# Gate and up on whole-number weights, with the scales applied when a bank is read, and down two tiles behind

## What is computed

```
xn = layernorm(x)                                  # 2048 rows of 512
s  = attention(xn)                                 # q, k, v projection, clip, layer norm of q and k,
                                                   # 32 heads of 16, ALiBi, causal softmax, output projection
W  = (imatrix - zeros) * scales                    # imatrix: integers 0..15; zeros and scales: one row per 128 input rows
g  = silu( (silu(xn @ W_gate) * (xn @ W_up)) @ W_down )     # 512 -> 1792 -> 512
out = x + s * g
```

## Time and profile before

| | us |
|---|---|
| median of 3 runs | 1297.69 (1294.58 to 1305.38) |
| span of the profiled execution | 1300.7 |
| stage 1, projection of q, k, v (to about 205) | 205 |
| stage 2, attention and weight jobs (about 205 to 764) | 559 |
| stage 3, output projection and feed-forward (about 764 to 1300.7) | 537 |
| TensorE busy | 1205.7 (93%) |
| VectorE busy | 754.4 (58%) |
| ScalarE busy | 626.0 (48%) |
| GpSimd busy | 503.3 (39%) |

### The profile page before, as it was taken

How to read it: one execution, slowest core, us unless ns; L and a number is a source line. 1 busy time by engine, 2 the same in 40 slices (tenths; PEclk the granted TensorE clock), 3 DMA queues, 4 the chain that set the end, 5 groups by cost and what they waited for, 6 DMA issues and landing times. The chain is left out here.

```text
span 1300.7 us, 23572 instructions
## 1 busy us (share of the span) xinstructions
PE 1205.7 (93%) x6848; PEld 768.9 (59%) x6848; DVE 754.4 (58%) x1835; ACT 626.0 (48%) x955; POOL 503.3 (39%) x544
## 2 busy tenths in 40 slices
PE   6999987999999899899998989999999999999997
PEld 5777752333333333333333358887888888888886
DVE  6877887877877778778777622225222522252223
ACT  3333332666666566566665764335433443344332
POOL 2755550313131221212131333555455445545553
PEclk9999986999999999999999989999999999999999
DMA  6234454454546444555565210001100010011000
GB/s 222 91 115 131 138 163 133 116 144 105 147 105 143 99 118 84 125 107 149 107 149 108 83 69 1 1 1 40 57 0 0 32 65 0 0 33 65 1 1 33
DMA packets 101901, 106.62 MB, mean 82 GB/s; under 512 B 28385, under 2 KB 81121, under 8 KB 101729
## 3 DMA queue, kind: packets, MB, share of 16 engines
q1 hardware_dynamic: 75392, 93.10, 27.7%
q10 hardware_dynamic: 26464, 12.98, 3.4%
HBM read 84.41 MB, written 21.23 MB: 81 GB/s over the span
## 5 line engine op out<-in xcount | busy, mean ns | idle before, releaser
L842 ACT ACTIVATE pr<-pair 128x1024 f32<-128x1024 f32 (+3 forms) x384 | 293.6, 811 | 179.7 <-PE pair L965 101.3
L1089 POOL TENSOR_TENSOR ws_lo<-w_f,ws_hi 128x512 fp32r<-128x512 f32 x168 | 238.0, 1445 | 271.8 <-ACT ws_hi L1130 271.8
L264 DVE CUSTOM_DVE_ANT_0 bank<-bank,sg 128x384 f32<-128x384 f32 (+3 forms) x512 | 242.3, 515 | 97.7 <-PE bank L274 94.4
L1251 DVE TENSOR_TENSOR sg<-pair,sg 128x512 f32<-128x512 f32 x56 | 38.8, 692 | 276.0 <-ACT sg L1188 276.0
L1318 PE MATMUL pair<-xc_hi,ws_lo 128*128 128x512 f32 x448 | 175.4, 392 | 0.0
L1318 PE MATMUL pair<-xc_lo,ws_hi 128*128 128x512 f32 x448 | 175.2, 391 | 0.0
L1318 PE MATMUL pair<-xc_hi,ws_hi 128*128 128x512 f32 x448 | 175.1, 391 | 0.0
L267 DVE TENSOR_REDUCE mx<-bank 128x1 f32<-128x512 f32 x256 | 159.8, 683 | 7.4 <-PE bank L274 6.7
L1188 ACT ACTIVATE sg<-pair 128x512 f32<-128x512 f32 x56 | 33.5, 598 | 235.7 <-PE pair L1318 235.6
L799 POOL TENSOR_TENSOR w_f<-w_f,zst 128x896 f32 (+1 forms) x24 | 50.1, 2088 | 215.2 <-ACT zst L856 215.2
L274 PE MATMUL bank<-xin_c,s_sb 108*128 108x512 bf16 (+3 forms) x384 | 118.3, 354 | 13.1 <-DVE mx L264 10.2
(11 more groups left out here) (101 smaller groups left out, 1980.0 us busy)
## 6 DMA issues: line engine op xcount, KB each, us to landing
stk<-parts ACTq DMA_DIRECT2D x16, 768.0 KB, 5.9
zst<-in_z_all SPq DMA_DIRECT2D x24, 448.0 KB, 4.2
sst<-in_s_all SPq DMA_DIRECT2D x24, 448.0 KB, 5.0
w_f<-in_w_all SPq DMA_DIRECT2D x24, 448.0 KB, 6.8
xin_c<-in_x SPq DMA_DIRECT2D x32, 256.0 KB, 2.7
s_sb<-stk SPq DMA_DIRECT2D x96, 64.0 KB
xin_c<-stk SPq DMA_DIRECT2D x96, 64.0 KB
qs<-stk SPq DMA_DIRECT2D x96, 64.0 KB
```

The lines of the kernel that those rows point to most:

```text
L264: dve.tensor_tensor_reduce(out=src, in0=src, in1=tri[:, 512 - w:512], scale=1.0, scalar=-3.0e38, op0=ALU.add, op1=ALU.max, accum_out=dst). ...
L842: act.activation(pr[e % 3][:, 2 * p:2 * p + 2, 0:w], pair[p][:, :, 0:w], ACT.Exp, scale=SCALE)\
L1089: return pool.tensor_tensor(dst, src, hi.bitcast(F32), ALU.subtract)
L1251: dve.tensor_tensor(sg[s][:, :], pair[s][:, 1, :], sg[s][:, :], ALU.mult).then_inc(h_mul, 1)
```

## The change

**Gate and up.** The half jobs of gate and up no longer multiply by the scales: GpSimd subtracts the zeros and writes the whole numbers (-15 to 15) straight into a tile of type F32R, `w_gu`, which holds them without a rest. Only down's weights (`w_d`) are still scaled. The scale DMA of those 16 of the 24 half jobs is gone (`sst` now takes their raw integers). `gate_up` is 2 matmuls for each projection and contraction tile, `xc_lo` and `xc_hi` against the same whole-number weights: 16 a tile of 128 channels in place of 24. Each of the 8 partial sums of a tile has a PSUM bank of its own, in a ring of four (`GB`), because its scale differs. The scale is a number per partition there, from a small tile `sgu` that stage 1 makes (one DMA, one transpose, one copy). The first contraction tile's sum is read by ScalarE (`first`: copy with scale into `acc`), the other three by VectorE (`add`: bank times scale plus `acc`, a scalar_tensor_tensor). silu and the product (`gate`) then work on `acc` in SBUF.

**Down.** `h_lo` is made on GpSimd (`h_low`) in place of VectorE, and of the weights only down's piece is split in stage 3 (one ScalarE copy and one GpSimd subtraction a tile in place of three each). On TensorE `gate_up` is cut in four pairs, and `down` of two tiles before in four quarters; they alternate.

**Around the blocks.** Attention's transposes go through the `y` banks, with split tiles of their own (`of_hi`, `of_lo`), and the output projection's halves stand between the pairs of tiles 0 to 2. xn has four buffers in place of two.

The core of the diff:

```diff
-                def job(jj):
-                    w = w_f[:, bass.ds(jj * HALF, HALF)]
-                    pool.wait_ge(z_conv, jj + 1)
+                def job(ip, n):
+                    w = w_half(ip, n)
+                    pool.wait_ge(z_conv, 3 * ip + n + 1)
                     apart(pool, "pool")
+                    if n < 2:
+                        pool.tensor_tensor(w_gu[:, bass.ds(half_of(ip, n) * HALF, HALF)], w, zst[:, :], ALU.subtract)\
+                            .then_inc(w_ready, 1)
+                        return
                     pool.tensor_tensor(w, w, zst[:, :], ALU.subtract).then_inc(z_sub, 1)
...
-                    pool.tensor_tensor(w, w, sst[:, :], ALU.mult).then_inc(z_mul, 1)
+                    pool.tensor_tensor(w, w, sst[:, :], ALU.mult).then_inc(w_ready, 1)
...
+                def h_low(b, it):
+                    pool.wait_ge(hh_done, IT * b + it + 1)
+                    pool.tensor_tensor(h_lo[it % 3][:, :], acc[0][it % 2][:, :], h_hi[it % 3][:, :].bitcast(F32), ALU.subtract)\
+                        .then_inc(hl_done, 1)
+                def w_low(b, it):
+                    pool.wait_ge(wd_high, IT * b + it + 1)
+                    pool.tensor_tensor(wd_lo[it % 2][:, :], w_down(it), wd_hi[it % 2][:, :].bitcast(F32), ALU.subtract)\
+                        .then_inc(wd_low, 1)
...
+                def first(b, it, n):
+                    act.wait_ge(hl_done, IT * b + it + 1)
+                    act.wait_ge(gu_done, IT * NJ * b + NJ * it + n + 1)
+                    act.activation(acc[n][it % 2][:, :], GB[n], ACT.Copy, scale=scale_of(n, 0, it)).then_inc(ev_first, 1)
...
                 def body(b, last):
...
+                    for it in range(IT + 1):
+                        if it > 0:
+                            silu(b, it - 1)
+                        if 1 <= it <= 2:
+                            copy_s(b, 2 * it - 2)
+                        if it < IT:
+                            for n in range(2):
+                                first(b, it, n)
+                        if it < 2:
+                            hi_o(b, 2 * it)
+                            load_o(b, 2 * it + 1)
+                        if it == 0:
+                            hi_o(b, 1)
+                            load_o(b, 2)
+                        else:
+                            h_high(b, it - 1)
+                            if it <= 2:
+                                copy_s(b, 2 * it - 1)
+                            if it == 1:
+                                hi_o(b, 3)
+                            w_high(b, it - 1)
...
+                def add(b, it, j):
+                    n, k = j % 2, j // 2
+                    dve.wait_ge(gu_done, IT * NJ * b + NJ * it + j + 1)
...
+                    dve.scalar_tensor_tensor(out=a, in0=GB[j % 4], scalar=scale_of(n, k, it), in1=a, op0=ALU.mult, op1=ALU.add)\
+                       .then_inc(ev_add, 1)
...
-                    for g in range(2):
-                        for k in range(KT):
-                            cols = slice(k * P, (k + 1) * P)
-                            for n, (l, r) in enumerate(terms(ws_hi[s][:, g, cols], ws_lo[s][:, g, cols], xc_hi[:, k, :], xc_lo[:, k, :])):
-                                mm = pe.matmul(pair[s][:, g, :], l, r, start=(k == 0 and n == 0), stop=(k == KT - 1 and n == 2))
-                    mm.then_inc(gu_done, 1)
...
+                        w = w_col(n, k, it)
+                        pe.matmul(GB[j % 4], w, xc_lo[:, k, :], start=True, stop=False)
+                        pe.matmul(GB[j % 4], w, xc_hi[:, k, :], start=False, stop=True).then_inc(gu_done, 1)
...
+                    for it in range(3, IT):
+                        for t in range(4):
+                            gate_up(b, it, t)
+                            down(b, it - 2, t)
+                    for t in range(4):
+                        down(b, IT - 2, t)
+                    if not last:
+                        for u in range(4):
+                            trans_x(b + 1, u)
+                    for t in range(4):
+                        down(b, IT - 1, t)
```

More of the change, by code:

```diff
@@ L819, in body @@
                     if s == 0:
-                        job(3 * ip + 1)
+                        job(ip, 1)
                 groups(pool, body)
@@ L1321, in down @@
-                def down(b, it):
-                    s = it % 2
-                    if it == 0:
-                        pe.wait_ge(s_cp, 4 * b + 4)
-                    pe.wait_ge(wd_lo, IT * b + it + 1)
-                    pe.wait_ge(hl_done, C_HL + IT * b + it + 1)
-                    for t in range(4):
-                        cols = slice(t * P, (t + 1) * P)
-                        for n, (l, r) in enumerate(terms(h_hi[s][:, cols], h_lo[s][:, cols], ws_hi[s][:, 2, :], ws_lo[s][:, 2, :])):
-                            mm = pe.matmul(y[t][:, :], l, r, start=(it == 0 and n == 0), stop=(it == IT - 1 and n == 2))
-                        if it == IT - 1 and t < 3:
-                            mm.then_inc(y_sum, 1)
-                    mm.then_inc(down_done, 1)
+                    if half == 1:
+                        mm.then_inc(s_proj, 1)
@@ new lines, in down @@
+                def down(b, it, t):
+                    if t == 0:
+                        pe.wait_ge(wd_low, IT * b + it + 1)
+                        pe.wait_ge(hl_done, C_HL + IT * b + it + 1)
+                    if it == 0:
+                        pe.wait_ge(s_cp, 4 * b + t + 1)
+                    cols = slice(t * P, (t + 1) * P)
+                    for n, (l, r) in enumerate(terms(h_hi[it % 3][:, cols], h_lo[it % 3][:, cols], wd_hi[it % 2][:, :], wd_lo[it % 2][:, :])):
+                        mm = pe.matmul(y[t][:, :], l, r, start=(it == 0 and n == 0), stop=(it == IT - 1 and n == 2))
+                    if it == IT - 1 and t < 3:
+                        mm.then_inc(y_sum, 1)
+                    if t == 3:
+                        mm.then_inc(down_done, 1)
```

303 lines of the change are left out of this document (156 added, 147 removed).

## The result

The changed kernel takes **1173.19 us** (median; 1171.58 to 1174.32) against 1301.37 of the kernel before on the same chip: a ratio of 0.901 (95% interval 0.8965 to 0.9054), 128 us less. Measured once more in another job (a job is one set of executions on one chip, always with the kernel before beside it) it took 1172.74 us, ratio 0.9024 (0.9002 to 0.9046). The forecast was 1197 us, range 1180 to 1222.

What follows compares the result with a forecast made beforehand. The prediction took TensorE to bound stage 3. Its terms: 1300.7 - 101.6 (matmuls) + 8.7 (block boundaries) - 2 (start of stage 3) - 6 (stage 2) = 1199.8 us, less 3.0 to the median: 1197 us, range 1180 to 1222.

Steps and rivals of the forecast that it cites:

- the term for stage 2: Stage 2: with 16 of 24 scale DMAs gone, ordinary waits for the dt DMA go: -6 us, ends 0 and -19.
- the term for stage 1: Stage 1: the small scale tile costs under 0.5 us.
- Removed matmuls, -101.6: Stage 3: 448 matmuls go at 0.2267 us each, -101.6 us if TensorE stays the bound; a tile takes 6.35 us.
- Added waits on TensorE, 0: Stage 3: eight waits a tile, already met, cost 0; the other end is 0.03 us each, 13 us.
- VectorE at 0.69 us an add: Stage 3: each of six scalar_tensor_tensor a tile takes 0.69 us; VectorE becomes the bound only above 0.94 us.
- the slower case, 1.37 us always: Stage 3 rival, chance 0.03: each scalar_tensor_tensor takes 1.37 us, VectorE needs 8.9 us a tile, 143 us more, 1340.
- The stalls, +8.7: Stage 3's block boundaries: three TensorE stalls per block, together 4.3 us; +8.7 us over all blocks against before.
- (a): Block start: TensorE's transpose waits for ScalarE's second load of attention's result, 3.0 us; 2.0 in the first block.
- (b): Block start: a later transpose waits for ScalarE's first copy, behind silu of tile 0 and a table load: 0.7 us.
- (c): Block end: down of tile 13 waits for the product, its split and the weights' low part: 0.6 us, 2.6 in the last.
- Stage 3 as a whole, -94.9: Stage 3: removed matmuls -101.6, block boundaries +8.7 and start of the stage -2 us.
- No rival came in: Four rivals outside the range, 0.20: clock falls 0.06, VectorE paces but faster 0.08, slower 0.03, gain lost to hand-overs 0.03.

Runs made afterwards that it cites:

- fewer DMAs alone: The kernel before with the 16 scale DMAs of the gate and up half jobs left out, GpSimd still multiplying: 1282.03 us, ratio 0.984.
- shifted kernel before: The kernel before with an unused tile of 448 bytes a partition ahead of sg0, no instruction changed: 1280.68 us, ratio 0.9872.

## Why the forecast was right in part and wrong in the sum

The steps that failed are two, both outside stage 3: the term for stage 2 (-6, measured -23.9 in the 14 groups) and the term for stage 1 (under +0.5, measured -7.4).

**Removed matmuls, -101.6: right.** The rate stayed and the tile is 6.35 us as forecast. The first two blocks stand 108.33 us apart where the text said 108.0 (839.18 and 947.51 are the first `down` matmuls of tile 13 in them); that this came so close is in part luck. A block's 440 matmuls are 99.8 us, which leaves 8.6. The text filled them with 4.3 of stalls and about 4 of transposes. The stalls are 2.4 (2.07 and 0.37), so 6.1 go to the transposes and the stream around them.

**Added waits on TensorE, 0: right.** Of the 448 matmuls that carry the waits only one was held, at the start of the stage, and the tile has no room for more than the 28 matmuls. The clock stayed at 0.99. The Trainium skill (TensorE: Matmul & The Clock Gate, "A second HAM failure mode: psum-queue depth-cycling") describes a kernel whose clock went up and down while it cycled through PSUM banks. Here banks were handed over every second matmul, and no run showed it in stage 3: 0.99 or 1.00 from 735 us on, with three more adds a tile too.

**VectorE at 0.69 us an add: 0.74 to 0.75 by duration, 0.66 by distance.** No effect, since some 1.7 us a tile were free. The form with a PSUM operand is indeed not slowed by GpSimd: while `h_lo` runs on GpSimd from 1001.01, VectorE's add reads 0.74 us, as without. Timeline after:

```profile
1000.83 0.75 DVE L1281 SCALAR_TENSOR_TENSOR gate<-pair,sgu,gate 128x512 f32<-128x512 f32 x1 [0.94 <-PE pair L1365]
1001.01 1.29 POOL L1135 TENSOR_TENSOR h_lo<-gate,h_hi 128x512 fp32r<-128x512 f32 x1 [3.79 <-ACT h_hi L1160]
1001.50 0.74 DVE L1281 SCALAR_TENSOR_TENSOR up<-pair,sgu,up 128x512 f32<-128x512 f32 x1
```

The text was wrong that the trace of before has no scalar_tensor_tensor. Stage 1 has it, in the same 128x512 with its operands in SBUF:

```profile
70.64 0.75 DVE L542 SCALAR_TENSOR_TENSOR qk<-qk,mvq,lnb 128x512 f32<-128x512 f32 x1
```

All 32 of that line have a median of 752 ns; the longest took 1573. So the row gives the form its ordinary time, and with it the slower case, 1.37 us always, had less to stand on.

**The stalls, +8.7: the mechanism right, the size half too large.** (a) was 0.53, 2.07, 2.07 and 0.64 us in the four blocks, where the text had 2.0 in the first and 3.0 in the others (1.7 in the last, which has no table load). (b) did not come; in the last block TensorE waited 0.84 us for `of_lo`, which the text did not have. (c) was 0.37, 0.38 and 0.38, where 0.6 was forecast, and 1.69 at the very end, where 2.6 was. The boundary in the timeline after:

```profile
836.54 1.28 POOL L1135 TENSOR_TENSOR h_lo<-gate,h_hi 128x512 fp32r<-128x512 f32 x1 [3.65 <-ACT h_hi L1160]
837.78 1.27 POOL L1140 TENSOR_TENSOR wd_lo<-w_d,wd_hi 128x512 fp32r<-128x512 f32 x1
839.18 0.49 PE L1375 MATMUL bank<-wd_hi,h_lo 128*128 128x512 f32 x1 [0.37 <-POOL wd_lo L1140]
840.18 2.72 ACT L1246 ACTIVATE sg<-bank 128x512 f32<-128x512 f32 x4
842.91 1.28 ACT L1191 ACT_TABLE_LOAD   x1
844.21 0.69 ACT L1191 ACTIVATE gate<-pair,sgu 128x512 f32<-128x512 f32 x1
845.84 0.64 ACT L1160 ACTIVATE oin_v<-o_sb 128x512 f32 x1
846.53 0.66 PE L1323 MATMUL bank<-ident,oin_v 128*128 128x128 f32 x4 [2.07 <-ACT oin_v L1160]
```

The four silus of y follow each other in 2.72 us. The text had the last two held by VectorE's products of 1.34 us and so put the last silu's end 1.5 us behind the last down; that was the step that failed in (a). It ended 0.7 us behind it (842.90 against 842.18), since only the first two products had to be done for the last two silus. The sum of (a) and (c) over the blocks is 5.3 + 2.8 us. The stalls of before, which the forecast subtracts, were also mis-sized: the text has 1.9 us a block, the timeline shows 0.40 and 0.63 to 0.74.

**Stage 3 as a whole, -94.9: measured -98.0.** 3 us off. Cut at the first `down` matmul of tile 13 in each block (before at 899.95 and 1290.49 us, after at 839.18 and 1160.20), the first piece, with the start of the stage, came out 28.5 us shorter, where -25.4 - 2 + 1.5 = -25.9 was forecast: 2.6 of the 3 us are there. The three blocks behind it came out 69.5 us shorter; -25.4 + 2.4 for each is -69.0.

**Stage 2, -6 with ends 0 and -19: wrong, -23.9.** Three faults. First, the long waits. The text took the ordinary ones, 6 to 7 us, and put the long ones at nothing because it could not tell. All of them went but the one of 4.0 us at the start of stage 2, which is in the 21.0 of the earlier trace rows and stands outside the 14 distances: the waits within them were 17.0 us before and 0 after. The other 7 us of the 23.9 I put to the clock, 0.97 before and 1.00 after over the stage; that is an estimate by subtraction. The run with fewer DMAs alone gave 20 us. Second, the bound. It took 33.53 us, the first of the 14 distances, as the least there is. That group has no wait for dt in it, but it is longer than the others are without theirs: after the change it takes 33.55 us and each of the others 33.0 to 33.3. The second group of before, less its own wait for dt (0.75), shows this:

```profile
311.90 0.72 ACTq L827 DMA_DIRECT2D qs<-dt  x1
```

311.90 - 277.96 - 0.75 = 33.19 us, which is just what the groups take after the change (464.71/14). The bound should have been 14 x (34.90 - 33.19) = 24 us. Third, the place of the tiles was not in the sum; it shortens the same groups (471.2 us in the shifted kernel before, with the whole load).

**Stage 1, under +0.5: wrong, -7.4.** The text costed what `sgu` does (a DMA, a transpose, a copy), not where it stands. No view of the profile of before shows the sign of that. But the two address classes, 64 and 192 bytes off a multiple of 256, could be read from the two built programs and weighed with the rule of the Trainium skill (DMA: Bandwidth & Descriptors, "How a descriptor splits into AXI transactions") named above; the text never looked at where the tiles stand, and had no rival for it.

**The range.** With the true stalls and 24 us for stage 2 the sum is 1300.7 - 98 - 24 - 0.9 = 1177.8, still over the measured 1170.4 by the 7.4 us of stage 1. The high end was not worked out rightly either: stage 2 unchanged is +6 and (a) to (c) half as long again is 4 x 4.3/2 = +8.6, which is +14.6 and not +12. No rival came in.

## What to carry to other kernels

Where one engine is the bound and its rate is even, the distance between two starts times the instructions removed gives the gain (101.6 us here, of which the boundaries of the blocks took back 3.6), provided every hand-over is laid out in one tile's timeline with its slack. Bound the gain of "waits removed" by the work without any wait: take each stretch less the wait in it, not the shortest stretch that the trace happens to have. And a new tile ahead of others is an edit of its own: look at the addresses modulo 256 bytes of what the DMAs touch, and measure the old kernel with an unused tile of the same size before giving its effect to the change.

## What the runs showed of the hardware that was not expected

- An unused tile of 448 bytes per partition made the kernel before 18 us faster (ratio 0.987, 0.981 to 0.993), one of 512 bytes did nothing, one of 64 bytes some 8 us. Stores of 768 KB landed after 4.9 to 5.2 us in place of 5.6 to 5.9 where their tiles began on a multiple of 256 bytes; there VectorE waited 9.1 us for the loads of x in place of 15.4.
- A small DMA issued behind a burst of two DMAs of 448 KB instead of three, in two of three jobs, was late 6.4 us in sum instead of 20.0, 3.7 and 4.0 of them at the start of stage 2; the clock over stage 2 was 0.97 before and 1.00 with both the smaller burst and the shift.
- Adds of 128x512 that read PSUM and SBUF read 0.74 us each but follow one another at 0.66 us.
- ScalarE's table loads in stage 3 went from 6 to 1 when its loop over the blocks was written out, at the same order of silu and copy.
